# The order of three engines' queues in the attention loop of a gated cross-attention block

## The reference, cut to what matters

```
x  = x + tanh(g_xattn) * attention(layernorm(x), ctx, ctx)   # B=4, S=1024, E=512, 16 heads of 32
x  = x + tanh(g_ffn)   * coupled_ffn(layernorm(x))
attention:
  scores  = Q K^T / sqrt(32) + adj[q,k];  -inf where mask == 0
  weights = softmax(scores)
  out     = (weights V) Wo^T + bo
```

## Time and profile before

| | |
|---|---|
| median of 3 runs | 1740.18 us (1739.29 to 1740.37) |
| the profiled execution's own time | 1739.29 us |
| its span | 1737.5 us |
| granted TensorE clock, mean | 0.998 |
| busy, share of the span: PE / PEld / DVE / ACT / POOL | 99% / 74% / 83% / 70% / 38% |

### The profile page before, as it was taken

One profiled execution on the slowest core, in us unless ns is written; L12 is line 12 of the kernel. 1 busy time (PEld: TensorE's weight loads), 2 busy tenths in 40 slices (PEclk: granted clock), 3 DMA queues, 4 the chain that ended last, 5 costly groups with the idle time before them and its releaser, 6 DMA issues. The chain is left out here.

```text
span 1737.5 us, 34186 instructions
## 1 busy us (share of the span) xinstructions
PE 1711.4 (99%) x12456; PEld 1292.6 (74%) x12456; DVE 1450.2 (83%) x2554; ACT 1220.7 (70%) x2185; POOL 660.5 (38%) x590
## 2 busy tenths in 40 slices
PE   9999999999999999999999999999999999999997
PEld 7888888777777777777777777777775685774863
DVE  6554545999999999999999999999678976868868
ACT  4222224999999999999999999999564365365455
POOL 3432342423278543586432875533235010100100
PEclk9999999999999999999999999999999999999999
DMA  7777675865468565567763686456403514221101
GB/s 278 273 252 276 242 265 145 197 180 129 142 166 188 126 148 130 137 209 149 147 156 114 186 180 139 118 111 159 155 16 93 170 42 120 88 74 49 64 1 49
DMA packets 152472, 254.65 MB, mean 147 GB/s; under 512 B 17024, under 2 KB 69504, under 8 KB 152320
## 3 DMA queue, kind: packets, MB, share of 16 engines
q1 hardware_dynamic: 101936, 158.78, 28.6%
q0 software_dynamic: 49808, 92.82, 23.8%
q10 hardware_dynamic: 576, 1.05, 0.2%
HBM read 168.44 MB, written 84.15 MB: 145 GB/s over the span
## 5 line engine op out<-in xcount | busy, mean ns | idle before, releaser
L1023 DVE CUSTOM_DVE_ANT_0 a_neg<-a_sc_ps,am 128x1024 f32<-128x1024 f32 x512 | 621.0, 1213 | 1.5 <-PE a_sc_ps L853 0.8
L963 ACT ACTIVATE a_prob<-a_neg,a_row_min 128x1024 f32<-128x1024 f32 x512 | 586.0, 1147 | 5.0 <-DVE a_row_min L1023 4.2
L867 PEld LDWEIGHTS a_tr_ps<-ident,a_prob 128*128 128x128 f32 x4096 | 468.2, 140 | 104.4 <-issue 52.9
L867 PE MATMUL a_tr_ps<-ident,a_prob 128*128 128x128 f32 x4096 | 538.1, 274 | 0.2
L998 DVE COPY a_probT<-a_tr_ps 128x512 f32<-128x512 f32 x512 | 351.3, 686 | 34.1 <-PE a_tr_ps L867 32.7
L941 ACT ACTIVATE a_probT<-a_tr_ps 128x512 f32<-128x512 f32 x512 | 302.5, 591 | 72.1 <-PE a_tr_ps L867 72.1
L749 POOL DMA_DIRECT2D a_q_st<-q_parts x144 | 79.4, 557 | 192.2 <-PE a_sc_ps L853 156.2
L853 PE MATMUL a_sc_ps<-k_first,a_q_st 96*128 96x512 f32 x384 | 135.7, 435 | 1.2 <-DVE a_row_min L1023 0.9
L853 PE MATMUL a_sc_ps<-a_k_st,a_q_st 96*128 96x512 f32 x384 | 135.6, 434 | 0.0
L887 PE MATMUL a_o_ps<-a_probT,a_v 128*32 128x256 f32 x2048 | 123.6, 382 | 0.6 <-ACT a_o L952 0.6
L887 PE MATMUL a_o_ps<-a_probT,v_first 128*32 128x256 f32 x2048 | 123.8, 382 | 0.0
(11 more groups left out here) (227 smaller groups left out, 3168.7 us busy)
## 6 DMA issues: line engine op xcount, KB each, us to landing
a_q_st<-q_parts POOLq DMA_DIRECT2D x144, 128.0 KB, 4.0
k_first<-k_parts POOLq DMA_DIRECT2D x24, 512.0 KB, 8.0
a_k_st<-k_parts POOLq DMA_DIRECT2D x24, 512.0 KB, 7.6
a_m_raw<-mask SPq DMA_DIRECT2D x24, 512.0 KB, 5.1
a_adj_raw<-adj SPq DMA_DIRECT2D x24, 512.0 KB, 5.9
k_parts<-p_out_hi SPq DMA_DIRECT2D x32, 256.0 KB, 5.4
k_parts<-p_out_lo SPq DMA_DIRECT2D x32, 256.0 KB, 6.4
v_all<-p_v_out SPq DMA_DIRECT2D x8, 1024.0 KB, 4.4
```

What stands on the lines that cost most here:

```text
L867: last = pe.transpose(tr_ps[:, bank(u, half), j * P:(j + 1) * P], prob[:, r % NPROB, t * P:(t + 1) * P], ident[:])
L963: act.activation(prob[:, r % NPROB, :], neg[:, r % 2, :], ACT.Exp, scale=-1.0, bias=row_min[:, r % 2:r % 2 + 1], accum_out=row_sum[:, r // ...
L1023: dve.tensor_tensor_reduce(out=neg[:, r % 2, :], in0=sc_ps[:, r % 2, :], in1=am[:, 2 * qb + qt, :], scale=-1.0, scalar=3.4e38, op0=ALU.add ...
```

## The change

All three versions of `step` get another order. PE's scores run up to one unit less ahead, two pairs of score matmuls stand together, the transposes form runs of three, three and two halves (12, 12 and 8 instructions) in place of two, three, two and one, both halves of a unit now belong to the same step, and `weighted_values` stands at the end of the step in place of its middle. `transpose_rinv` moves from `r % 32 == 4` to `r % 32 == 8`, ahead of the step's last scores. ACT's `weights` run up to four units ahead in its step and both engines' `read_transposes` follow in other places; DVE's `read_rinv` moves from the end of the step `r % 32 == 8` to the second quarter of the step `r % 32 == 12`. The number and shapes of all instructions inside the loop stay as they are, as do buffers, semaphores and DMAs.

```diff
@@ -897,30 +897,28 @@   (PE)
             def step(p, r):
-                scores(*shifted(p, r, 4))
-                if p or r:
-                    transposes(*shifted(p, r, -1), 1)
+                scores(*shifted(p, r, 3))
                 transposes(p, r, 0)
-                scores(*shifted(p, r, 5))
                 transposes(p, r, 1)
                 transposes(p, r + 1, 0)
+                scores(*shifted(p, r, 4))
+                scores(*shifted(p, r, 5))
                 transposes(p, r + 1, 1)
+                transposes(p, r + 2, 0)
+                transposes(p, r + 2, 1)
+                if r % UG == UB:
+                    transpose_rinv(2 * p + r // UG, isinstance(p, int) and p == 0 and r < UG)
                 scores(*shifted(p, r, 6))
+                transposes(p, r + 3, 0)
+                transposes(p, r + 3, 1)
                 for n in range(QUAD):
                     weighted_values(p, r + n)
-                transposes(p, r + 2, 0)
-                transposes(p, r + 2, 1)
-                scores(*shifted(p, r, 7))
-                transposes(p, r + 3, 0)
-                if r % UG == QUAD:
-                    transpose_rinv(2 * p + r // UG, isinstance(p, int) and p == 0 and r < UG)
-
-            for r in range(4):
+
+            for r in range(3):
                 scores(0, r)
-                for n in range((0, 6, 5, 0)[r]):
+                for n in range((0, 6, 5)[r]):
                     pe.matmul(o_ps[:, 0:P], ident[:], ident[:], start=True, stop=True)
             run(step)
-            transposes(NPAIR - 1, PAIR - 1, 1)
@@ -966,18 +964,17 @@   (ACT)
             def step(p, r):
-                weights(p, r)
                 weights(p, r + 1)
-                read_transposes(*shifted(p, r, -2))
                 weights(p, r + 2)
-                read_transposes(*shifted(p, r, -1))
                 read_transposes(p, r)
+                read_transposes(p, r + 1)
                 weights(p, r + 3)
-                read_transposes(p, r + 1)
-
+                read_transposes(p, r + 2)
+                weights(*shifted(p, r, 4))
+                read_transposes(p, r + 3)
+
+            weights(0, 0)
             run(step)
-            read_transposes(NPAIR - 1, PAIR - 2)
-            read_transposes(NPAIR - 1, PAIR - 1)
@@ -1027,14 +1024,19 @@   (DVE)
             def step(p, r):
-                for n in range(QUAD):
-                    negated(p, r + n)
-                    read_transposes(*shifted(p, r, n - 4))
-                    if r % UG == UB and n == 3:
-                        read_rinv(2 * p + r // UG, isinstance(p, int) and p == 0 and r < UG, o_ps[0:UG, QB:QB + P])
+                negated(p, r)
+                read_transposes(*shifted(p, r, -3))
+                read_transposes(*shifted(p, r, -2))
+                if r % UG == UB + QUAD:
+                    read_rinv(2 * p + r // UG, isinstance(p, int) and p == 0 and r < UG, o_ps[0:UG, QB:QB + P])
+                negated(p, r + 1)
+                negated(p, r + 2)
+                read_transposes(*shifted(p, r, -1))
+                negated(p, r + 3)
+                read_transposes(p, r)
 
             run(step)
-            for k in range(4, 0, -1):
+            for k in range(3, 0, -1):
                 read_transposes(NPAIR - 1, PAIR - k)
```

## The result

The changed kernel takes 1754.92 us (median of 4 runs, 1753.62 to 1756.28), the kernel before 1739.74 beside it (4 runs, 1739.29 to 1740.37). The ratio is 1.0087, 95% interval 1.0069 to 1.0104: the new order is slower by 0.9%. The forecast was 1743.9 with a range of 1731 to 1753, so the time lies outside it, close to the third rival (a new wait in every step, 1756 and more). The profiled execution of after took 1753.87 us, its span is 1752.1, and the mean granted clock is 0.997 against 0.998, so PE's clock has no part that could be seen.

A forecast was written before the change was run, and what follows sets the result against it. PE was taken to bound the attention loop. Its new order was to add 6.3 us and the sums' transpose to save 2.6, +3.7 in all with no new ordinary wait: 1743.9 us, range 1731 to 1753.

The forecast's parts named there:

- the third rival: Transposes of u+3: a new wait in every step, on the chain with 0.15 slack; 1756 us and more, chance 0.15.
- Do new waits appear?: Part of the prediction that timed all engines through the new step: no wait in an ordinary step.
- An engine sees a group's end 0.04 after it: Hand-over from PE to a waiting engine: assumed 0.04 us after the end of a group of transposes or scores.
- slack 0.15: Before the transposes of u+3: DVE's copy u+1 done at 3.84 us, bank needed at 4.00; called the tightest place.
- the forecast's edges: Around the product with V: uncovered load behind it costs transposes little (0.85 against 0.80), scores about 0.11 us.
- +0.05 a step: PE's own work in the new order: 7.40 against 7.36 us, taken as +0.05; 126 steps give +6.3 us.
- item 5: From the product with V to the transposes behind the next step's scores: 1.86 + 0.57 = 2.43 us, bounds 2.33 and 2.52.
- The first rival: Product to scores: score weights load hidden behind the product, 2.33 us there, step 7.31, whole about 1731 us; chance 0.2.
- The term of the sums' transpose: Steps with transposed sums: DVE's copy of them moves before its free time, saving 0.17 us 15 times, -2.6 us.
- The reciprocal: Steps where DVE has a reciprocal more: DVE 0.26 late at copy u, 0.15 absorbs part, PE loses about 0.1 us.
- PE has 0.5 us of waits for DVE in the same stretch, all before scores: Reading of the old kernel's waits in mid-attention (800 us), used to conclude that PE bounds the loop.
- PE's work stays equal: Rival on PE's step: edges even out and the order only absorbs DVE's extras, -2.6 us, 1737.6 us; chance 0.17.

The follow-up runs named there:

- experiment 1: Changed kernel with both lists of waits turned: `negated` lists the scores first, PE's half-0 transposes DVE's copy first; 1743.46 us, 1.0022 to the kernel before.
- experiment 4: Changed kernel with DVE's copies of half 1 cut to three of four key tiles, the fourth zeroed at the start; 1743.31 us, 1.0020 to the kernel before.
- experiment 7: Changed kernel with the product with V ahead of the transposes of u+3, `transpose_rinv` and the reads placed to fit; 1737.93 us, 0.9993 to the kernel before.
- Experiment 8: Kernel before with DVE's `read_rinv` moved from the end of step `r % 32 == 8` behind the first `negated` of step `r % 32 == 12`; 1738.37 us, 0.9993.
- experiment 2: Changed kernel with the list of waits turned for DVE's `negated` alone; 1744.04 us, 1.0022 to the kernel before.
- experiment 11: Kernel before with the product with V moved behind both halves of the transposes of u+2, followed by scores u+7; 1764.57 us, 1.0145.
- experiment 3: Changed kernel with the list of waits turned for PE's half-0 transposes alone; 1748.09 us, 1.0045 to the kernel before.
- experiment 12: Kernel before with the product behind the transposes of u+2, and both lists of waits turned as well; 1753.34 us, 1.0080 to the kernel before.

## Why the prediction was wrong

**The step that failed** is in "Do new waits appear?": "An engine sees a group's end 0.04 after it", and from it "`negated` u+3 at 0.21 [...] slack 0.15. This is the tightest place", "So no wait in an ordinary step". The place was the right one, the size of the links was not. The 0.04 holds where the last semaphore to come is the one on the instruction itself (experiment 1: 0.04 on DVE, 0.05 on PE). In the changed kernel it is one of those ahead, and it takes 0.15 and 0.12. Along the chain that binds, from the end of scores u+4, that is 0.11 more at `negated` u+4 and 0.08 more at the load; 0.01 is the way from `negated` to the copy (1.15 for 1.14), and 0.03 lies between the late load and its first matmul (808.70 to 808.73), which the plan had at nothing. Together some 0.22 on a slack of 0.15: the transposes of u+3 begin 0.07 late (0.61 for 0.54). The lateness at `negated` u+3, which the plan's chain begins with, costs nothing here.

The rows of before could not warn of the first of these: there DVE hardly ever stood idle before `negated` (1.5 us of idle time in 512 of them), and from 400 to 1200 us no `negated` started sooner than 0.18 after the end of its scores, so what the queue did ahead of it was hidden by the instruction that ran. The change took that cover away: it moved DVE's idle time from before a copy, which has one wait, to before `negated`, which has two, and it brought the scores of u+4 just ahead of the place where `negated` needs them.

**What it cost.** The wait: 1754.92 - 1743.46 = 11.5 us, 0.09 a step. In the timelines this is 0.60 or 0.63 for 0.55 before the transposes of u+3, and 0.99 for 0.97 behind them. The rest of an ordinary step, 7.42 to 7.43 against 7.36, is the forecast's edges.

**The sum of the forecast.** +0.05 a step was nearly right: experiments 1 and 4 show +0.06 to +0.07, experiment 7 shows that it is the product's place. Its heart, item 5, came out as planned, 2.43 (804.66 - 802.23), with scores that begin with an uncovered load. The Trainium skill, "TensorEngine Tiling (Array Packing)", Key Properties, has a change of mode drain the engine. The trace agrees at the product's new edge: 0.41 without a load, as at the old one. So by this rule alone the step would have stayed at 7.36; it went to 7.42. The other rule of the Trainium skill that was weighed, the early loading of weights in "TensorE: Matmul & The Clock Gate", Part 2, step-by-step part, isn't seen at this edge: the load comes 1.86 after the product's start. The first rival falls by the 2.43, where it had 2.33. The term of the sums' transpose held too: forecast -0.17 x 15 = -2.6. Experiment 8 shows 2.24 by the steps, some 0.15 each, and in experiment 1 that step is 0.10 to 0.11 over its neighbours (7.53 and 7.42 to 7.43), which is PE's own 0.11. (In after it is as long as its neighbours, because PE's extra 0.11 covers the new wait there: the transposes of u+3 follow after 0.54.) The two together and without the wait are the kernel of experiment 1: 1743.46, where the forecast said 1743.9. That it is so close is partly luck: the edges took some 2 us more than forecast, and the step with the reciprocal gave back about 1 that the sum did not have.

**The reciprocal.** Forecast: PE loses about 0.1. Measured: 7.66 - 7.53 = 0.13 against its neighbours, 0.16 against the ordinary steps of its own kind (7.50), and 0.07 in experiment 1, where no other wait stands in the way.

**A reading.** "PE has 0.5 us of waits for DVE in the same stretch, all before scores" leaves out loads of the product that the same view puts down to DVE (19.0 us, 54 times, above). The conclusion stands: there is such a stretch once in every step, whoever is named.

**The rivals.** That PE's work stays equal (1737.6) is refuted by 7.42 in experiments 1 and 4. The new wait, given 0.15, happened at its place, and at its price: with some 0.09 a step it is between "no wait" and the first full tenth, on top of the forecast. Its chance was too low. The argument against it, "every link has its own row", was true of the durations of the instructions and not of the times between them.

**What stays open.** Every second ordinary step is some 0.03 longer in after (7.49 and 7.52). The records show where this arises: in these steps u+4 is the first unit of a block, and its `negated` has a third wait. It starts 0.176 after its scores in place of 0.147, and the semaphore instruction ahead of it, which now waits for two semaphores, takes 0.050 in place of 0.021. In experiments 1 and 2 the difference is gone. That the third wait is the cause was argued from this; no experiment changed it alone. The records also split the delays. On DVE the semaphore instruction starts 0.042 after the scores' end, takes 0.021, and `negated` starts 0.084 later. On PE it starts 0.040 after the copy's end, takes 0.051, and the load starts 0.025 later. What the engines do in the 0.084 and 0.025 is not shown.

## What to carry to other kernels

A slack of 0.15 us on a chain with two hand-overs between engines (PE to DVE, DVE to PE) was no slack here: price each hand-over at a place where the receiving engine really stands idle with the same number of waits, and not where its queue was hidden by work. Where an instruction waits for several semaphores, write the one that comes last first; here it was worth 11.5 us where the chain was tight, 11.2 in another tight order, and nothing where it wasn't. Before an order is changed for the busiest engine, look in the steps that are longer than their neighbours: moving two small DVE operations gave 0.22%, while the new order of the busiest engine's queue gave nothing at best.

## What the runs showed of the hardware that was not expected

- The delay from a hand-over to the start of the next instruction depended on the order of the waits: on DVE 0.15 us after the end of the scores against 0.04, on PE 0.12 after the end of the copy against 0.05.
- A late load of transposes was put down to "issue" in after, to an exponential in experiment 11 and to the copy in experiments 3 and 12. In each case the copy ended last. In after the exponential had ended 0.79 us or more before the load in every step from 400 to 1200 us, in experiment 11 at least 0.38. With several waits the name in the row depended on how the waits were written.
- A 128x64 memset of 0.11 us between an accumulator read and a copy moved the copies' end by about 0.02 us.
- Scores behind the product begin with an uncovered load: 0.56 to the transposes behind them, where a further pair within a group adds 0.44 to 0.46.
